# A gated attention and FFN layer on one core: another order of the first score group, and output multiplications ahead of operand splits

## The reference, cut to what matters

```python
# x, ctx: (64, 128, 512); 4 heads of 128; INTER = 1408
def xattn(x, c):                          # x is layernorm(x)
    Q, K, V = x_h @ Wh, c_h @ Wh, c_h @ Wh            # the same Wh per head
    masked = Q @ K.T / sqrt(128) * decay              # per head, 128 x 128
    A = maximum(abs(masked.sum(axis=0)), 1)           # summed over all 64 batches
    O = A @ V
    Y = (O - mean) / sqrt(var + 1e-3) * gamma + beta
    return (relu(x @ wg) * Y) @ wo
x = x + tanh(g_xattn) * xattn(layernorm(x), ctx)
h = layernorm(x)
x = x + tanh(g_ffn) * ((silu(h @ gate.T * gs) * (h @ up.T * us)) @ down.T * ds)
```

## Time and profile before

| | |
|---|---|
| median of 3 runs | 1519.28 us (1518.38 to 1520.39) |
| profiled execution | 1518.46 us |
| its span | 1516.7 us |
| TensorE busy | 1495.3 us, 99% of the span |
| VectorE busy | 1060.0 us, 70% |
| ScalarE busy | 680.8 us, 45% |
| GpSimd busy | 718.5 us, 47% |
| DMA engines | 66.9% of the span, 305.94 MB |

### The profile page before, as it was taken

How to read it: one execution, slowest core, us unless ns; L and a number is a source line. 1 busy time by engine, 2 the same in 40 slices (tenths; PEclk the granted TensorE clock), 3 DMA queues, 4 the chain that set the end, 5 groups by cost and what they waited for, 6 DMA issues and landing times.

```text
span 1516.7 us, 20330 instructions
## 1 busy us (share of the span) xinstructions
PE 1495.3 (99%) x7226; PEld 1255.6 (83%) x7226; DVE 1060.0 (70%) x1501; ACT 680.8 (45%) x1063; POOL 718.5 (47%) x767
## 2 busy tenths in 40 slices
PE   6999999999999999999999999999999999999998
PEld 5888888888888888888888888888788888888887
DVE  7677788788557676666676767564777778778672
ACT  4444434445544535455354545534344344343442
POOL 4556666771444535435453534434137237137236
PEclk9999999999999999999999999999999999999999
DMA  6888788776778687777876887676372473562422
GB/s 234 276 262 266 261 289 280 258 235 211 222 231 233 193 244 210 190 245 207 252 204 179 244 231 231 176 212 156 115 215 105 124 215 109 138 203 94 140 97 84
DMA packets 374647, 305.94 MB, mean 202 GB/s; under 512 B 258384, under 2 KB 284368, under 8 KB 374352
## 3 DMA queue, kind: packets, MB, share of 16 engines
q1 hardware_dynamic: 374544, 304.61, 66.9%
HBM read 200.23 MB, written 117.31 MB: 209 GB/s over the span
## 4 chain that ended last, share of the span: by engine, by line
PE 86%; DVE 4%; DMA 3%; POOL 3%; issue 1%; ACT 1%; SPq 1%; DVEq 0%; POOLq 0%; ACTq 0%
PE ps L1703 37%; PE po L1703 8%; PE pyb L1582 8%; PE ptb L1703 5%; PE pyb L1703 5%; PE ps L1617 5%; PE po L1582 5%; PE pyb L1687 3%; PE ptb L1687 3%; PE pyb L1691 2%; PE ptb L1691 2%; PE ptb L1587 1%; PE ps L1582 1%; SPq L439 1%; DMA v_scratch<-tmp 1%
## 5 line engine op out<-in xcount | busy, mean ns | idle before, releaser
L1411 POOL TENSOR_SCALAR rs<-mv 128x1 f32<-128x1 f32 (+1 forms) x132 | 52.8, 400 | 298.7 <-DVE mv L1057 148.0
L1501 POOL TENSOR_TENSOR reg<-tmp,reg 128x512 fp32r<-128x512 f32 x88 | 117.5, 1336 | 124.7 <-ACT reg L730 124.7
L1582 PE MATMUL pyb<-reg,xreg 128*128 128x512 f32 x708 | 176.0, 396 | 0.6 <-DVE xreg L961 0.6
L1703 PE MATMUL ps<-reg,gate 128*128 128x512 f32 x704 | 174.8, 390 | 1.4 <-DVE tmp L1190 0.8
L1703 PE MATMUL ps<-reg,up 128*128 128x512 f32 x704 | 173.9, 389 | 0.0
L1703 PE MATMUL ps<-op,wbuf 128*128 128x512 f32 x704 | 173.9, 389 | 0.0
L1703 PE MATMUL ps<-xreg,reg 128*128 128x512 f32 x704 | 163.4, 390 | 1.3 <-DVE tmp L1190 1.3
L1481 POOL TENSOR_TENSOR p5b<-p5b,p1b 128x512 f32<-128x512 f32 x44 | 57.1, 1299 | 217.7 <-ACT p5b L754 217.7
L1703 PEld LDWEIGHTS ps<-xreg,reg 128*128 128x128 f32 x704 | 131.5, 188 | 29.1 <-DVE tmp L1190 1.8
L1703 PEld LDWEIGHTS ps<-op,wbuf 128*128 128x128 f32 x704 | 132.1, 188 | 27.4
L1703 PEld LDWEIGHTS ps<-reg,up 128*128 128x128 f32 x704 | 132.1, 188 | 27.4
(11 more groups left out here) (154 smaller groups left out, 2827.9 us busy)
## 6 DMA issues: line engine op xcount, KB each, us to landing
wbuf<-ws_scratch SPq DMA_DIRECT2D x44, 896.0 KB, 4.7
xr<-in_x SPq DMA_DIRECT2D x63, 512.0 KB, 5.5
raw<-in_ctx_t SPq DMA_DIRECT2D x32, 512.0 KB, 4.6
w_scratch<-tmp SPq DMA_DIRECT2D x64, 256.0 KB, 4.8
v_scratch<-tmp SPq DMA_DIRECT2D x64, 256.0 KB, 4.0
raw<-v_scratch SPq DMA_DIRECT2D x32, 512.0 KB, 6.6
x_scratch<-xr SPq DMA_DIRECT2D x32, 512.0 KB, 4.6
xr<-x_scratch SPq DMA_DIRECT2D x32, 512.0 KB, 6.1
```

Source lines behind the costliest of these rows:

```text
L1501: e.tensor_tensor(hid[1][:, m % 11, :], tmp[:, m % 3, :], f(hid[0][:, m % 11, :]), ALU.subtract).then_inc(s["hlo"])
L1582: last = e.matmul(dst, lhs[a], rhs[b], start=(k == 0 and i == 0), stop=(k == n - 1 and i == 2))
L1703: last = e.matmul(dst, l, r, start=(k == 0 and i == 0), stop=(k == n - 1 and i == 1), skip_group_check=sums)
```

## The change

Seven things are changed, and no arithmetic among them.

- The third and fourth x tile are loaded apart, with a semaphore of its own (`xs`) for the third; the identity goes behind the second x.
- Wh and its transpose are loaded into `turned[0]` (`wh_first`), no longer into `xr`; so the load of the seventh and eighth x waits for nothing, and GpSimd's weight sums, which later write there, wait for G and for the split of Wh.
- wg is loaded ahead of the context and of Wh. The identity, wg and Wh apart, the order of the first loads is kept. The small loads of columns and rows go behind group 0.
- Group 0 is written out on SP, ScalarE, VectorE and TensorE. TensorE does xt 0, xt 1, G, xt 2, xt 3, and then gate products k by k between the z products, and later transposes between the halves of v. ScalarE and VectorE take their part of the wg split between those of the third and fourth tile and of G. SP issues the first copy of the FFN weights (704 KB, HBM to HBM) behind two V stores.
- GpSimd waits for VectorE's first wg split before its first context split, and `rstd(4)` goes between its two context splits.
- In all eight FFN groups the second pair's x2 split stands at step 14, and `x_again` is piece 7.
- In `prepare` the second difference goes from stage 0 to stage 1.

```diff
@@ sync @@
             def x_load(q):
-                if q == 3:
-                    p.wait_ge("whlo", 1)
-                    p.wait_ge("G", 1)
...
             e.dma_start(xr[:, 0, :], x_v[:, 0, :]).then_inc(s["xf"], 16)
+            e.dma_start(xr[:, 1, :], x_v[:, 1, :]).then_inc(s["xl0"], 16)
             e.dma_start(ident[:, :], eye).then_inc(s["eye"], 16)
-            e.dma_start(xr[:, 1, :], x_v[:, 1, :]).then_inc(s["xl0"], 16)
-            e.dma_start(xr[:, 6, :].rearrange("p (h n) -> p h n", h=4), wh_t.rearrange("h e d -> e h d")).then_inc(s["whr"], 16)
-            x_load(1)
+            e.dma_start(xr[:, 2, :], x_v[:, 2, :]).then_inc(s["xs"], 16)
+            e.dma_start(xr[:, 3, :], x_v[:, 3, :]).then_inc(s["xl1"], 16)
+            e.dma_start(wh_first[0], wh_t.rearrange("h e d -> e h d")).then_inc(s["whr"], 16)
+            e.dma_start(tmp[:, :, :], wg.rearrange("(k p) n -> p k n", p=128)).then_inc(s["wgr"], 16)
             ct_load(0, 1)
-            e.dma_start(xr[:, 7, :].rearrange("p (h n) -> p h n", h=4), wh.rearrange("h d e -> d h e")).then_inc(s["whr2"], 16)
+            e.dma_start(wh_first[1], wh.rearrange("h d e -> d h e")).then_inc(s["whr2"], 16)
             ct_load(0, 0)
             x_load(2)
-            e.dma_start(tmp[:, :, :], wg.rearrange("(k p) n -> p k n", p=128)).then_inc(s["wgr"], 16)
             x_load(3)
+            ct_load(1, 0)
+            ct_load(1, 1)
+            w_store(0)
+            w_store(1)
+            x_load(4)
+            v_store(0)
+            v_store(1)
+            weights_chunk(0)
+            v_store(2)
+            w_store(2)
+            v_store(3)
+            x_load(5)
+            ct_load(2, 0)
...
-                        if piece == 6:
+                        if piece == 7:
                             x_again(q)
@@ scalar @@
             xt_hi(0)
             xt_hi(1)
+            xt_hi(2)
+            wg_hi(0)
+            xt_hi(3)
+            wg_hi(1)
             p.wait_ge("G", 1)
             e.copy(g4[0], pz[0]).then_inc(s["Ghi"])
-            xt_hi(2)
-            xt_hi(3)
+            wg_hi(2)
+            wg_hi(3)
+            z_hi(0)
             ct_first(0)
             ct_first(1)
+            p.wait_ge("whr2", 16)
+            e.copy(whs[:, 0, :, :], wh_first[1]).then_inc(s["whhi"])
+            z_hi(1)
+            w_out(0)
+            z_hi(2)
+            xt_hi(4)
+            z_hi(3)
+            w_out(1)
...
-                    if g + 1 < NS and step == (13 if g else 14):
+                    if g + 1 < NS and step == 14:
                         x2_pair_hi(2 * g + 3)
@@ vector @@
             norm(1)
             stats(3)
+            norm(2)
             xt_lo(0)
-            norm(2)
+            norm(3)
             xt_lo(1)
-            norm(3)
+            xt_lo(2)
+            wg_lo(0)
+            xt_lo(3)
             p.wait_ge("Ghi", 1)
             e.tensor_tensor(g4[1], pz[0], f(g4[0]), ALU.subtract).then_inc(s["Glo"])
+            wg_lo(1)
+            wg_lo(2)
+            stats(4)
+            wg_lo(3)
+            z_lo(0)
...
                 if stage == 0:
                     operand_lo(m, 0)
                     combine(m, 0)
-                    combine(m, 1)
                 if stage == 1:
                     operand_lo(m, 3)
+                    combine(m, 1)
                     combine(m, 2)
...
-                    if g + 1 < NS and step == (13 if g else 14):
+                    if g + 1 < NS and step == 14:
                         x2_pair_lo(2 * g + 3)
@@ gpsimd @@
             rstd(3)
+            p.wait_ge("wglo", 1)
             ct_split(0, 2)
+            rstd(4)
             ct_split(0, 3)
-            rstd(4)
@@ tensor @@
             xt(0)
+            xt(1)
             p.wait_ge("whr", 16)
...
             last.then_inc(s["G"])
-            xt(1)
             xt(2)
             xt(3)
+            w(0, (0,))
+            z(0)
+            w(0, (1,))
+            z(1)
+            w(0, (2, 3))
+            z(2)
+            w(1, (0,))
+            z(3)
+            w(1, (1,))
+            xt(4)
+            w(1, (2, 3))
+            v(0, 0)
+            v(1, 0)
+            v(0, 1)
+            w(2, (0, 1))
+            xt(5)
+            v(1, 1)
+            v(2, 0)
+            xt(6)
+            v(2, 1)
+            w(2, (2,))
+            xt(7)
+            w(2, (3,))
+            v(3, 0)
+            v(3, 1)
```

143 lines of the change are left out of this document (70 added, 73 removed).

## The result

The kernel after takes 1511.27 us in the median of 4 runs (1510.51 to 1512.21), where 4 runs of the kernel before, beside it, took 1519.38 (1518.38 to 1520.39): 8.1 us less, a ratio of 0.9946 [0.9931, 0.9962]. The forecast was 1514.2, the range 1511.6 to 1518.3; the time lies 0.3 under its low end. The profiled execution took 1512.21, with a span of 1510.4.

What follows compares the result with a forecast made beforehand. TensorE was taken to bound the kernel, with 21.4 us idle. Front 3.0, combine 1.3 and x2 split 0.8 sum to 5.1 us: 1518.46 profiled becomes 1513.4, plus 0.8 to the median gives 1514.2, range 1511.6 to 1518.3.

Steps and rivals of the forecast that it cites:

- The front, 3.0 us: First 40 us: first product 1.8 us earlier, 1.46 of waits covered, 0.3 of new waits; group 1 at about 36.5.
- 1.46 - 0.3: Group 0 after its first product: gate products cover waits of 0.27, 0.61 and 0.58 us; new mid-group waits cost 0.3.
- the fourth rival: The front's order only moves its waits; front gives 1 us or less, time 1516.2 to 1517.2; chance 0.10.
- The clock, 0 within 0.9: TensorE's half-rate stretch in the front: loss unchanged, term taken as zero, with 0.9 us lost or won as bounds.
- The combine, 1.3 us: Later FFN, near 1060 us: second difference behind the output multiplication removes TensorE's wait, 1.3 us.
- The x2 split, 0.8 us: Fifth FFN group: split one step later stands behind the output multiplication, removing TensorE's wait of 0.81 us.
- the re-read at nothing: FFN: re-read of x one step later frees SP's y and x2 transfers from waiting behind it; priced at no cost.
- The gate weight: Rival: the gate weight lands late and holds the front; time 1515.5, or 1518.0 if as late as before; chance 0.12.
- took no wait's place: Rival: in FFN groups two to seven the later x2 split delays the next group's first product; 1523.4 us; chance 0.07.
- no FFN wait only moved: Rival: the FFN's waits only move, hanging on late transfers, so the front alone counts; 1516.3 us; chance 0.16.
- Coalescing: Rule weighed for the front's x loads: splitting one transfer delays everything behind by 0.5 us, so the front gives 2.5.
- The slowdown of VectorE beside GpSimd: Rule weighed at about 14 us: a weight split loses up to 1.3 us beside POOL's context split; 0.7 would show.

Runs made afterwards that it cites:

- e9: The kernel before, unchanged, run and profiled once more: 1519.99 us.
- e2: The kernel before with only the three FFN edits (x2 split, re-read of x, second difference): 1514.96 us, ratio 0.9963 to before.
- e17: The kernel before with the x2 split moved to step 14 and the re-read of x to piece 7: 1516.94 us, ratio 0.9978 to before.
- e6: The kernel after with only the second difference put back in stage 0: 1513.13 us, ratio 0.9946 to before.
- e4: The kernel after with only the second pair's x2 split put back at step 13: 1516.31 us, ratio 0.9965 to before.
- e18: The kernel before with only the combine's move (second difference from stage 0 to stage 1): 1517.1 us, ratio 0.9985 to before.
- e1: The kernel after with its three FFN edits undone, so the new front alone: 1516.63 us, ratio 0.9969 to before.
- e14: The kernel before with only the re-read of x moved to piece 7: 1519.62 us, ratio 0.9992 to before.
- e7: The kernel after with the third and fourth x tile loaded by one 512 KB transfer again: 1512.06 us, ratio 0.9941 to before.
- e3: The kernel after with only the re-read of x put back at piece 6: 1513.0 us, ratio 0.9952 to before.
- e5: The kernel after, unchanged, run once more: 1510.8 us, ratio 0.9931 to before.
- e16: The kernel after with group 0's first z products in one block and 7 useless identity products in front: 1516.09 us, ratio 0.9971 to before.

## Why the prediction was wrong

*The front, 3.0 us.* The sum was right, its terms were not, and that they cancel is luck. Over the profiled executions the first mark lies at 383.59 to 385.13 in the seven kernels with the old front, 384.1 in the mean, and at 380.49 to 381.48 in the six with the new one, 381.0: 3.1 us. The first product of group 0 starts at 16.5 in the mean of the seven (16.05 to 17.39) and at 14.2 in the six (13.41 to 14.78): 2.4 us where I had 1.8. From there to group 1 it is 23.1 us (23.07 to 23.45) and 22.4 (21.80 to 22.73): 0.7 where I had 1.46 - 0.3. The 1.46 was misread. Of the three waits in the earlier trace rows only that of 0.27 was for the evacuation of z (L953). The 0.61 stood before a gate product and was for a split of the gate weight (L961), and the 0.58 before the eighth transpose, for its norm (L944). A gate product between z products covers only the first. In the kernel after the 0.61 is gone, z waits 0.59, and the seventh and eighth transpose wait 0.33 and 0.60 for VectorE's split of the transpose before: 1.52 us in place of 1.46. The first of these splits stood in VectorE's list behind a norm that had waited 0.94 us for its root, until 30.08, as forecast; the second behind a norm that took 1.53 us. Idle time before 40 us came to 10.6, not to the 9 that I had named as a sign. For the waits the fourth rival was right.

*The clock, 0 within 0.9.* In the profile the full level came 3.75 us after the first product in place of 5.7, at the end of my bounds that wins, and it may be the source of the 0.7. But that is one draw. With the old front the four z products ran at the half level to the last in e9, and only for the first two, 3.2 us, in e2 and e17; with the new one it was nothing in e6 and 5.3 us in e4. That the change shortens this stretch is not shown.

*The combine, 1.3 us.* The mechanism was right, the size 1.65: the wait of 1.35 and some 0.3 beside, as e6 shows. The VectorE queue behind it was no worry, since the second difference took 1.21 us out of GpSimd's way; the multiplication after it stood at 1061.35.

*The x2 split, 0.8 us, and the re-read at nothing.* **This is the step that failed.** "Both cost nothing" looked at what the later re-read would harm, and not at what the early one was holding up: in the first FFN group it held the x2 loads, by them ScalarE, and by it TensorE for 0.7 to 1.6 us, in a row of TensorE's waits that the profile of before already had. The two edits together took the middle from 664.6 to 666.2 (four executions, mean 665.2) down to 662.5: **2.7 us where I had 0.8**. I had also priced the split's wait as the one seen, where TensorE waits for a landing that varies from one execution to the next. It was 0.8 to 1.1 us with both edits undone (before, e9, e18, e1) and 2.25 and 2.61 with the re-read's edit alone (e4, e14), where the clock's fall came on top.

*The basis.* I added the 0.8 between the profiled execution and the median unexplained. That execution had the shortest middle of the four, with e18's. So part of what lay between it and the median may have been in waits that the change removes, and the median could gain more than the profile showed; no run without a trace can show it. The range's low end had no working either: my terms go 0.9 below the sum, to 1513.3, not to 1511.8.

The sum by the marks is 3.1 + 2.7 + 1.65 = 7.5 us, against 8.1 measured (5.8 to 10.5 by the ratio's interval). Front alone and FFN alone, 4.0 and 5.7 by medians, are 9.7, within the same uncertainty. That the two halves act on each other was not shown.

*The rivals.* The gate weight did not hold the front: its first split stood at 12.62 on VectorE, as written, and what TensorE waited for was the fourth tile's. The x2 split at step 14 took no wait's place, and no FFN wait only moved, in the whole change; in e14 it did just that. *Two rules.* Coalescing: the Trainium skill (DMA: Bandwidth & Descriptors, Rules for kernel authors) advises to join many small transfers into a large one. In e7 neither the landing nor the time tells one load from two. The slowdown of VectorE beside GpSimd is seen here too: two weight splits at 14.63 took 1.87 us beside a GpSimd split at 14.06, where two like them took 1.28 us in the kernel before, at 20.95, with GpSimd idle. That cost TensorE nothing, as it did not wait for them. But the same slowdown did show at another place, which I had not priced. In the middle of group 0, the norm at 31.74 took 1.53 us instead of 0.54, beside a GpSimd split at 31.70 (1.41 to 1.54 us in e1, e3, e4 and e6, 1.39 in e5). ScalarE's cast for VectorE's next split was done at 32.62, and that split, for which the eighth transpose waits 0.60 us, began at 33.19; so by my estimate nearly all of that wait is the slow norm's.

## What to carry to other kernels

Read what a queue's waiting instruction is holding up, engine by engine, before pricing its move at nothing. Each wait of the bounding engine in the profile needs a named cause, even the small ones, and the releaser in the brackets says whether a change can reach it. When two waits in a row hang on transfers, removing one alone may only bring the engine to the next sooner. To divide a gain of a few us, compare marks with the same work behind them across many profiled executions, rather than medians that scatter by 1 us.

## What the runs showed of the hardware that was not expected

- TensorE's granted clock fell to half after a single wait in dense work that had run at the full level: after 2.25 us (e4, 0.53) and 2.61 us (e14, 0.59, eight matmuls in 3.38 us), and after 2.08 and 1.25 us close together (e16, 0.50). In e4 that made the wait cost 1.6 us more than it lasts. It stayed full after 1.34 (e6) and 1.57 us (e1). The Trainium skill (TensorE: Matmul & The Clock Gate, Part 1: The HAM clock gate) has half rate as the default that activity lifts, and the rows agree.
- In the front the length of the wait does not settle it: behind 2.16 us (kernel after) the products ran at half, behind 1.75 us at half in e4 and at full in e6. The column of the granted clock does not show it either: it reads 1.00 from 14.3 to 19.6 us in e4, where the products of three matmuls start 1.28 to 1.45 us apart, and 1.00 in e6, where it is 0.7 to 0.8. The spacing of like matmuls does.
- A wait costs more than it shows even at the full level: 1.34 us of wait moved the end by 1.67, 0.16 of it before the idle time that the trace counts and 0.18 in the matmuls behind it.
- VectorE's difference of two 128x1024 tiles took 3.30 us at 1051.71, while GpSimd made a split of the same size, and 1.21 at 1058.89, when GpSimd's had ended (at 1057.28).
